# Another order of TensorE's steps in a two-layer conv and Mamba kernel on one core

## The reference, cut to what matters

```python
def reference(x, ...):                                  # x: 16 x 64 x 64 x 96, float32
    # layer 0: alias-free pointwise MLP
    x = x + layer0(_gn(x))      # upsample 2x (Fourier), 96 -> 384, a + b*h + c*h*h, 384 -> 96, low pass, every 2nd
    # layer 1: Mamba over the 4096 tokens of a sample
    x = x + layer1(_gn(x))
...
def layer1(u):                                          # d_inner 192, d_state 16, dt_rank 6
    xs, z = split(u @ W_in.T)
    xc = silu(causal_conv3(xs) + conv_b)
    dt, Bm, Cm = split(xc @ W_x.T)
    delta = softplus(dt @ W_dt.T + b_dt)
    h[t] = exp(delta[t] * A) * h[t-1] + delta[t] * Bm[t] * xc[t]    # 192 x 16 states
    y = (sum over states of h * Cm) + xc * D
    return (y * silu(z)) @ W_out.T
```

## Time and profile before

| | |
|---|---|
| device time, median of 3 runs | 7185.96 us (7182.05 to 7199.08) |
| the profiled execution | 7219.16 us, its span 7217.5 us |
| mean granted TensorE clock | 0.912 |
| PE busy | 6447.3 us (89%) |
| DVE busy | 5943.6 us (82%) |
| ACT, POOL busy | 4794.1 us (66%), 4577.4 us (63%) |

### The profile page before, as it was taken

One profiled execution on the slowest core, in us unless ns is written; L12 is line 12 of the kernel. 1 busy time (PEld: TensorE's weight loads), 2 busy tenths in 40 slices (PEclk: granted clock), 3 DMA queues, 4 the chain that ended last, 5 costly groups with the idle time before them and its releaser, 6 DMA issues. The chain is left out here.

```text
span 7217.5 us, 97516 instructions
## 1 busy us (share of the span) xinstructions
PE 6447.3 (89%) x32099; PEld 3299.1 (46%) x32099; DVE 5943.6 (82%) x4956; ACT 4794.1 (66%) x7986; POOL 4577.4 (63%) x4516
## 2 busy tenths in 40 slices
PE   7898998999898998999999899998999989898765
PEld 5545444444444444444444444444444444444211
DVE  0188888888888888888888888888888888889898
ACT  4576767667676776766667666676766767667554
POOL 0166666666666766667666666666766666677676
PEclk8998989999898998999999898998989999899776
DMA  3465655655655555565655555666555655555552
GB/s 89 112 151 134 146 141 129 148 136 146 148 136 141 140 143 137 145 147 131 150 130 147 143 134 140 138 150 144 136 146 132 150 137 145 144 129 142 121 122 68
DMA packets 805815, 983.15 MB, mean 136 GB/s; under 512 B 391258, under 2 KB 417542, under 8 KB 805318
## 3 DMA queue, kind: packets, MB, share of 16 engines
q1 hardware_dynamic: 805318, 976.92, 56.4%
HBM read 717.71 MB, written 259.00 MB: 135 GB/s over the span
## 5 line engine op out<-in xcount | busy, mean ns | idle before, releaser
L1069 POOL TENSOR_TENSOR hc<-hs,cs 128x512 f32<-128x512 f32 x3072 | 3843.5, 1269 | 2272.8 <-DVE hs L1028 1880.1
L1028 DVE TENSOR_TENSOR_SCAN hs<-av,state,b 128x512 f32<-128x512 f32 x2688 | 3282.4, 1264 | 83.5 <-DVE b L1022 2.7
L1022 DVE TENSOR_TENSOR b<-rep_u,pb 128x1536 f32<-128x1536 f32 x1024 | 1802.8, 1761 | 785.3 <-PE pb L746 721.2
L883 ACT ACTIVATE av<-rep_d,nega 128x512 f32<-128x512 f32 x3072 | 2129.2, 713 | 139.4 <-DVE hs L1028 134.9
L757 PE MATMUL py<-hc,rsel 128*32 128x512 f32 x6144 | 1227.4, 678 | 27.3 <-POOL hc L1069 27.2
L676 PEld LDWEIGHTS cb<-w2c,g 128*98 128x98 f32 x9600 | 937.6, 178 | 330.2 <-issue 267.9
L671 PE MATMUL cb<-xu,w1a 96*128 96x392 f32 x2400 | 1039.9, 529 | 50.1 <-ACT dlt L873 31.0
L676 PE MATMUL cb<-w2c,g 128*98 128x96 f32 x9600 | 990.2, 264 | 83.2 <-issue 55.4
L833 ACT ACTIVATE g<-cb,b1a 128x392 f32<-128x392 f32 x1200 | 695.7, 580 | 205.3 <-PE cb L671 189.5
L746 PE MATMUL pb<-bc,selb 96*128 96x512 bf16 x1024 | 416.4, 407 | 370.0 <-DVE b L1022 368.6
L710 PE MATMUL cb<-xn,wtap 96*96 96x512 f32 x1536 | 701.0, 606 | 0.3 <-DVE spare L966 0.3
(11 more groups left out here) (102 smaller groups left out, 6525.5 us busy)
## 6 DMA issues: line engine op xcount, KB each, us to landing
rep_d<-delta_scratch SPq DMA_DIRECT2D x512, 384.0 KB, 6.2
rep_u<-deltax_scratch SPq DMA_DIRECT2D x512, 384.0 KB, 6.1
cs<-c_scratch SPq DMA_DIRECT2D x512, 256.0 KB, 6.1
delta_scratch<-dlt SPq DMA_DIRECT2D x128, 384.0 KB, 3.1
deltax_scratch<-dlt SPq DMA_DIRECT2D x128, 384.0 KB, 8.1
t_scratch<-t1s SPq DMA_DIRECT2D x128, 300.0 KB
t1r<-t_scratch SPq DMA_DIRECT2D x160, 240.0 KB, 5.0
rr<-v_scratch SPq DMA_DIRECT2D x256, 150.0 KB
```

Of the source, the lines that this page charges most:

```text
L883: act.activation(av[:, n % NAV, :], rep_d[:, k % 2, j, :], ACT.Exp, scale=nega[:, q, j:j + 1])\
L1022: dve.tensor_tensor(b3[:, :, :], rep_u[:, k % 2, 3 * hf:3 * hf + 3, :], pb[:, None, :].broadcast_to([128, 3, T]), ALU.mult).then_inc(dve_b ...
L1028: dve.tensor_tensor_scan(hs[:, n % NHS, :], av[:, n % NAV, :], b3[:, n % 3, :], start, ALU.mult, ALU.add)\
L1069: pool.tensor_tensor(hc[:, n % NHC, :], hs[:, n % NHS, :], cs[:, k % 2, g % NQ, :], ALU.mult)\
```

## The change

Nothing is computed in another way. What changes is where the steps stand in the plan, and the slots in `AT`:

- The W steps are not spread evenly any more. `level` adds up PE's time in each three slots, with the price of each step from a table in the code, and puts W steps where the sum is low. W_HEAD goes from 62 to 68.
- X, X, Z stood at slot 8 of the chunk and Z at 9. Now X is at 8, Z at 9, X at 11 and Z at 12. No W, S or D step stands at slots 8 to 12.
- DBC moves from 13 to 16, DT from 17 to 21, OUT from 6 to 19.
- POOL's bc moves from (16, 21) to (18, 22). SP's dl moves from 20 to 22, du from 4 to 5, ru about one slot later, the output's store and the load of x1o (`out`) from 13 to 22.
- The stretch between the parts of a sample shifts: S steps end at 91 (before 84), D steps begin at 95 (96), WG stands at 106 (100), W of the next sample begins in earnest at 109 (105).

```diff
+OUT_AT = 19
...
-    "pool": dict(u=23, bc=(16, 21)),
-    "sp": dict(rd=(1, 2, 3, 5), ru=(6, 8, 10, 12), cs=(15, 16, 17, 18), dl=20, du=4, x1=21, out=13),
+    "pool": dict(u=23, bc=(18, 22)),
+    "sp": dict(rd=(1, 2, 3, 4), ru=(7, 9, 11, 13), cs=(15, 16, 17, 18), dl=22, du=5, x1=22, out=22),
...
-W_HEAD = 62
+W_HEAD = 68
+PE_US = {"ST": 0.46, "SA": 0.72, "SB": 0.72, "W_up": 0.73, "W_f": 0.73, "W_2": 2.27, "W_dn": 0.8, "D_lo": 1.4, "D_hi": 1.4,
+         "X": 2.73, "Z": 0.87, "DBC": 1.76, "DT": 0.53, "OUT": 3.05}
...
 def even(steps, lo, hi):
-    free = [p for p in range(lo, hi + 1) if not BATCH <= p % NU < BATCH + 2]
+    free = [p for p in range(lo, hi + 1) if not BATCH <= p % NU < BATCH + 5]
...
+def level(steps, lo, hi, rows):
...
+    base = {p: scans_us(p) for p in range(lo, hi + 1)}
+    for p, st in rows:
+        if lo <= p <= hi:
+            base[p] += PE_US.get(st[0], 0.2)
+    groups = {}
+    for p in range(lo, hi + 1):
+        groups.setdefault((p - 1) // 3, []).append(p)
+    for limit in range(300, 1200, 5):
+        out, todo = [], list(steps)
+        for slots in groups.values():
+            room = limit / 100 - sum(base[p] for p in slots)
+            share = room / len(slots)
+            for i, p in enumerate(slots):
+                while todo and not BATCH <= p % NU < BATCH + 5 and room >= PE_US[todo[0][0]] / 2 and room > share * (len(slots) - 1 - i):
+                    room -= PE_US[todo[0][0]]
+                    out.append((p, todo.pop(0)))
+        if not todo:
+            return out
...
 def mamba_rows(k, z_only=False):
     at = k * NU + BATCH
-    x = [] if z_only else [("X", k, 0), ("X", k, 1)]
-    rows = [(at, st) for st in x + [("Z", k, 0)]] + [(at + 1, ("Z", k, 1))]
-    return rows + ([] if z_only else [(at + 5, ("DBC", k)), (at + 9, ("DT", k, 0)), (at + 9, ("DT", k, 1))])
...
+    rows = [(at + 1, ("Z", k, 0)), (at + 4, ("Z", k, 1))]
+    return rows + ([] if z_only else [(at, ("X", k, 0)), (at + 3, ("X", k, 1)), (at + 8, ("DBC", k)),
+                                      (at + 13, ("DT", k, 0)), (at + 13, ("DT", k, 1))])
```

More of the change, by code:

```diff
@@ L69, in d_steps @@
     return [(h, k) for k in range(NC8) for h in ("D_lo", "D_hi")]
-W_HEAD = 62
+W_HEAD = 68
+PE_US = {"ST": 0.46, "SA": 0.72, "SB": 0.72, "W_up": 0.73, "W_f": 0.73, "W_2": 2.27, "W_dn": 0.8, "D_lo": 1.4, "D_hi": 1.4,
+         "X": 2.73, "Z": 0.87, "DBC": 1.76, "DT": 0.53, "OUT": 3.05}
+PE_PB, PE_RED, PE_SKIP = 0.28, 1.12, 1.03
 OFFSET = {"S": 2, "D": 1}
 def even(steps, lo, hi):
-    free = [p for p in range(lo, hi + 1) if not BATCH <= p % NU < BATCH + 2]
+    free = [p for p in range(lo, hi + 1) if not BATCH <= p % NU < BATCH + 5]
@@ L78, in even, with scans_us @@
     return [(free[i * len(free) // len(steps)], st) for i, st in enumerate(steps)]
+def scans_us(p):
+    n = p % NU
+    red = (n - AT["pe"]["red"]) % 3 == 0
+    first = (n - AT["pe"]["red"]) % NU in (0, 12)
+    return PE_PB * (n % 3 == AT["pe"]["pb"]) + PE_RED * red + PE_SKIP * first
+def level(steps, lo, hi, rows):
[17 more added lines that the diff above has]
+            return out
+    raise ValueError("the steps find no place")
@@ L81, in mamba_rows @@
 def mamba_rows(k, z_only=False):
     at = k * NU + BATCH
-    x = [] if z_only else [("X", k, 0), ("X", k, 1)]
-    rows = [(at, st) for st in x + [("Z", k, 0)]] + [(at + 1, ("Z", k, 1))]
-    return rows + ([] if z_only else [(at + 5, ("DBC", k)), (at + 9, ("DT", k, 0)), (at + 9, ("DT", k, 1))])
-def stage_rows(s, w_head, w_tail, d):
+    rows = [(at + 1, ("Z", k, 0)), (at + 4, ("Z", k, 1))]
+    return rows + ([] if z_only else [(at, ("X", k, 0)), (at + 3, ("X", k, 1)), (at + 8, ("DBC", k)),
+                                      (at + 13, ("DT", k, 0)), (at + 13, ("DT", k, 1))])
@@ L89, in stage_rows @@
+def stage_rows(s, w_head, w_tail, d, beside=()):
     rows, w = [], w_steps()
     if s:
-        rows += [(0, ("SLD", 0))] + even(s_steps(), 3, 84) + [(90, ("SG1", 0)), (95, ("SG2", 0))]
-    if w_head:
[L93 to L97, removed]
+        rows += [(0, ("SLD", 0))] + even(s_steps(), 3, 91) + [(96, ("SG1", 0)), (101, ("SG2", 0))]
+    if d:
+        rows += [(89, ("DLD", 0)), (93, ("DG", 0))] + even(d_steps(), 95, 133) + [(138, ("DG1", 0)), (143, ("DG2", 0))]
+    if w_tail:
+        rows += level(w[W_HEAD:], 0, 87, rows + list(beside))
+    if w_head:
+        rows += [(95, ("WLD", 0)), (106, ("WG", 0))] + even(w[:2], 101, 103)
+        rows += level(w[2:W_HEAD], 109, NC8 * NU - 1, rows + list(beside))
@@ L107, in plan_of @@
 def plan_of(kind):
-    rows = stage_rows(kind in ("first", "full"), kind in ("first", "full"), kind in ("first", "full", "tail"),
-                      kind in ("first", "full", "tail"))
+    rows = []
     for k in range(NC8):
@@ L114, in plan_of @@
             rows += mamba_rows(k, True)
-        rows.append((k * NU + 6, ("PAD", -1) if kind == "first" and k == 0 else ("OUT", k)))
+        rows.append((k * NU + OUT_AT, ("PAD", -1) if kind == "first" and k == 0 else ("OUT", k)))
     if kind == "last":
-        rows.append((NC8 * NU + 6, ("OUT", NC8)))
-    return padded(rows)
+        rows.append((NC8 * NU + OUT_AT, ("OUT", NC8)))
+        return padded(rows)
+    ahead = kind != "tail"
+    return padded(stage_rows(ahead, ahead, True, True, rows) + rows)
 def plan_before():
```

## The result

The changed kernel took 7240.01 us (7216.75 to 7259.93, 10 runs) against 7188.72 us for the kernel before: a ratio of 1.0063, 95% interval [1.0048, 1.0078]. It is a little slower, by more than the 0.3% that the prediction took as the limit. The forecast was 6865 us. The profiled execution has a span of 7244.3 us. It took 6 us more than the median of its kernel, that of the kernel before 30 us more than its own, so the difference between the two profiles (35 us over samples 0 to 13) is smaller than that between the medians (51 us).

The account below looks back on a forecast made before the run. PE's uneven work, coupled to DVE through one pb bank, was taken as the bound. DVE's 384 + 18 (DT) + 6 (between parts) + 6 (overshoots) = 414 us a sample against 434.8, so 323 us off 7186: 6863, say 6865; range 6690 to 7050.

Parts of the forecast that it names:

- The work per group: Between two spreads, the larger of PE's priced work and DVE's, summed over 64 groups: 428 us a sample before, 403.5 after.
- X, X, Z, Z cost 27 of the 51 us in this way, and the change removes nearly all of that: Group whose spread comes behind X and Z: 27 us a sample lost before, nearly all removed by the change.
- ACT at slot 14 must now wait for Z at PE's slot 12: Among moves without a price: ACT's wait costs nothing, as av 15 is not wanted for some 5 us after.
- So DVE waits 2.3 us: Chunk's end, behind DT's banks: DVE waits 2.3 us in the second chunk, 18 us a sample over all eight.
- PE goes cold in each wait: Rival: PE's clock may fall while waiting for DT's banks, 12 us a sample more; 7030 us, or 6950 with half; chance 0.22.
- the prediction's signs of being wrong: Groups behind X stay over 7 us, POOL holds up DVE, or the mean clock falls below 0.912.
- then ACT may do mid: Start of DT's chain: after POOL's product of slot 18 and B's difference at 3.7 us, ACT does `mid` till 4.3.
- I go by the rows: ACT's table switch: 1.28 us to the next activation, no drain; by the skill's page the 18 us would be near 28.
- Between the parts: Stretch between the parts of a sample: 11 us of loss before, 6 us a sample kept after.
- Moves without a price: OUT at 19, SP's `out`, x1 and dl at 22, and ACT's wait at slot 14: no cost given.
- Delta comes too late: Rival: POOL's delta * x waits for DT and delays DVE; gain gone at 2.9 us slip, 7310 us at 4; chance 0.09.
- No effect: Rival: DVE's waits only move from X's group to DT's; 7186 us within 0.3%; chance 0.04.

Follow-up runs that it names:

- e12: The changed kernel with X, X, Z at slot 8 and Z at 9 again, W allowed in slots 10 to 12, bc still (18, 22): 7090 us, 0.9855.
- e2: The changed kernel with only POOL's bc back at (16, 21): 7125 us, 0.9888 of the kernel before.
- e3: The changed kernel with W steps spread evenly over the free slots again, W_HEAD still 68: 7817 us, 1.0839 of the kernel before.
- e5: The changed kernel with bc back at (16, 21), X, X, Z at slot 8, Z at 9, and W allowed in slots 10 to 12: 7024 us, 0.9751.
- e9: The changed kernel with bc back at (16, 21) and X, X, Z at 8, Z at 9, but W, S, D kept off slots 8 to 12: 7082 us, 0.9843.
- e1: The changed kernel with DBC back at 13, DT at 17, and POOL's bc and SP's dl, du, ru, rd, x1 as before: 7410 us, 1.0298.
- e4: The kernel before with only X at 8, Z at 9, X at 11, Z at 12, and W, S, D kept off slots 8 to 12: 7325 us, 1.0165.
- e7: The changed kernel with bc back at (16, 21), OUT back at slot 6 and the output's store at 13: 7264 us, 1.0089 of the kernel before.
- e8: The changed kernel with bc back at (16, 21), DT at slot 19, OUT behind it at 20, dl and x1 at 21: 7098 us, 0.9853.
- e6: The kernel before with only W placed by PE's time (`level`) over the same slots, W_HEAD 62: 7212 us, 1.0016.

## Why the prediction was wrong

Three steps failed. The sample's time was taken from the larger of PE's and DVE's work in each group, by which the split of X and Z is a gain; undone alone, it gives 2.1% back (e12). DT's wait was set at 18 us where the groups it falls in now lose 35. And the move of bc, and ACT's wait behind X and Z, were put at nothing; bc costs 1.7% (e2).

**What bounds the kernel.** That PE and DVE are coupled by the one pb bank held, and PE's 365 us at the full clock were right (367 to 372 in all runs worked out above). But the prediction then counted from DVE's 384 us and added stalls, as if PE had 19 us to spare. It has them only when it neither idles nor runs at 1.2 GHz. Idle time of 27 to 38 us and 20 to 41 us of low clock stayed in every version worked out above, and more in e3.

**The work per group.** The step "X, X, Z, Z cost 27 of the 51 us in this way, and the change removes nearly all of that" was right at its place: 71 to 47 us. What failed is to take the sum of the larger of PE and DVE, group by group, for the sample's time. That sum sees how much work stands between two spreads and not whether PE may start it. By that sum the split is a gain of 9 us (413 with X and Z together, 403.5 apart, otherwise the same), and measured it is a loss of 7 (420.4 in e5, 427.5 in e2). e9 is plainer still: with the prediction's own prices the sum puts it some 21 us a sample over e2 (an estimate, worked out as the prediction did), and it measured 3 us under it (424.5 against 427.5). Keeping W off five slots of 24 (e9 against e5) and the split itself (e2 against e9) both cost. How much of each is the clock and how much the waits was not taken apart.

**ACT behind X and Z.** The prediction saw that "ACT at slot 14 must now wait for Z at PE's slot 12" and asked only whether av would be late for DVE. It put at nothing what ACT holds up for PE: the banks of the steps behind Z. That is the 2.16 us wait shown above and 10.5 us of PE's idle time a sample. In all seven kernels that make the last Z at slot 12 (the changed one, e1 to e4, e7, e8) PE waits 5.1 to 12.8 us a sample for ACT in the sixth groups; in all seven that make it by slot 9 (before, e5, e6, e9 to e12) it waits 0.

**DT.** The term of the sum that was most wrongly sized is the one that begins "So DVE waits 2.3 us" and ends in 18 us a sample. It set 18 against some 9 before; the first two groups of the chunks hold 35 us over DVE's pace against 8, that is 27 more. The heavy group at the seam took 11.14 us as forecast. The count took POOL as free for the product of slot 18, and POOL waits for PE's reductions 850.7 us in the run; and it took every step behind DT at the full clock. The latter is the rival "PE goes cold in each wait", which had been given 12 us a sample and 0.22. The low clock's term rose from 31.5 to 33.5 us a sample instead of falling, and e2 took 9.6 us of it away. One of the prediction's signs of being wrong so came true, by a hair: the mean clock was 0.911, under 0.912. The Trainium skill warns of such swings (TensorE: Matmul & The Clock Gate, A second HAM failure mode: psum-queue depth-cycling). The trace agrees that they occur in a kernel whose PE is busy 92% of the samples' time, and has 10.43 us at 0.60 against 6.04 at 1.00 for the same steps; that the small waits for banks start them is not shown here.

**bc.** The chain in the prediction begins with "then ACT may do mid", after POOL's slot 18, and yet the move of bc from 16 to 18 has no term of its own. It cost 115 us by the medians and 126 by the ratios (e2), over a third of the whole gain that was forecast. This wait was in the sum of DT and never compared with the place before. What it costs is shown by e2; that it costs by way of ACT's late evictions and PE's clock is what the timelines of slots 165 to 167 show for the place that gained most, and argued for the rest.

**Tables.** "I go by the rows" held: 3024.01 to 3025.31 is 1.30 us from the load to DT's first eviction. The drain of 1380 ns that the Trainium skill adds (ScalarE: Activation LUTs, What ACT_TABLE_LOAD costs) is not seen there.

**Between the parts.** 6 us of loss was taken. The window at slots 102 to 104 is 8.95 us at 0.66 where it was 13.86, but the two ahead of it take 16.5 us where they took 14.4, so slots 96 to 104 gave 2.9 us of the 5 counted.

**Moves without a price.** OUT's was good: e7 makes it worth 2%. But D steps wait for the load of rr, 96 us where it was 11, and 5.5 us a sample. The moved slots of SP seem not to be the cause: e1 put dl, du, ru, rd and x1 back and waits 104 us, e7 put the output's store back and waits 72, while e4 and e6, which leave the stretch between the parts as before, wait 12 and 8. So it comes with that stretch's new places, which no run changed alone.

**The rivals.** "Delta comes too late" did not decide: POOL waits 308 us for it, e2 still has 248 with the time 1.7% down, and e8 takes all but 43 of that away and gains only 0.4%. (The count of that rival has a slip: 11.3 + 3.1 is 14.4 and not 14.7.) "No effect" had it that DVE's waits only move, and gave it 0.04; that is close to what the groups show, but the way was another, with new waits of PE for ACT and of DVE for others than pb, and more time lost than won. Nor are 721 us of DVE's wait 51 a sample: 678.5 of them fall in the 14 samples, which is 48.

**What stays open.** Why DT at 17, with DBC and SP's slots back too, costs 4% against 21 when X and Z are apart (e1 against e2). Its sum over groups is 407 against 403.5, which doesn't explain it. And what starts each fall of the clock: the low clock's places move with the plan, but no run holds PE's order fixed and changes the clock alone.

## What to carry to other kernels

When one engine feeds another through a single buffer and both are near their limit, moving work away from the worst wait is not a gain by its size: ask first where that work goes, and what has to be emptied before it may start there. Slots kept free for one kind of work are paid for in all others. Give a term of its own to every number that is moved, above all to one that sets when a third engine may go on; here two steps on POOL, two slots and one slot later, cost 1.7%. And where an engine empties banks in order, ask for each of its waits not only who needs its own result next, but which banks stand behind it.

## What the runs showed of the hardware

The same three slots with the same steps took 6.04 us with PE at 1.00 and 10.43 us at 0.60, and the difference between the two kernels was two steps on POOL, two slots and one slot earlier. In fourteen samples, versions with the same idle time of PE (35 us a sample in the changed kernel and in e2) had 33.5 and 23.9 us of low clock: the amount of idle time alone does not set the clock. Nor does a single wait: one of 2.52 us was followed by a W_2 of 3.29 us in the one kernel and of 2.32 us, the full clock's time, in the other.
